# The count product of a routed expert layer: operands on 16 partitions, or on all 128

## The chip, the cores and the metric

One core of one Trainium2 chip runs the whole kernel. The metric is the device time of one execution in microseconds, over several runs; the profile is of one further execution. TensorE (PE) has its own queue, with weight loads shown apart (PEld); VectorE is DVE, ScalarE is ACT, GpSimd is POOL, and SyncE (SP) issues most DMAs.

## The reference, cut to what matters

```python
h = tokens(x, W, class_token, pos_embed)            # 16 images, 197 rows each
h = concatenate([h, txt], axis=1)                   # 16 x 325 rows of 192
h = h + attention(layernorm(h))                     # decay mask, no softmax
y = layernorm(h).reshape(T, 192)                    # T = 5200
sig = sigmoid(y @ Wg.T)                             # 128 experts
topk_idx = top_k(sig + e_bias, 6)                   # 6 experts for each row
order = argsort(topk_idx.reshape(-1))               # rows of each expert in order
pos = arange(P) - starts[se]                        # place within the expert
# each expert takes its first CAP = 192 rows
gu = einsum('ech,ehf->ecf', y[token_buf], W_gate_up)
yb = einsum('eci,eih->ech', silu(g) * u, W_down) * w_buf
out = h + scatter_add(yb) + silu(y @ Wsg) * (y @ Wsu) @ Wsd
```

## The kernel before, in words

The kernel has two stages. The image stage runs over 16 images: patch product, attention, layer norm, router logits, choice of six experts. For each image TensorE's `running_counts` (L1105) turns the 0/1 choices into a running count of rows per expert, and ScalarE makes of it `countT` (experts x 326), which is stored as row `crow[e, image, :]` in DRAM. A column holds 200 less the count so far, so the last column of an image is the first of the next.

The expert stage finds the rows of each active expert from these counts. SP's `load_counts` brings `crow[e]`, a tile of 16 images x 326 columns in bf16, to one of two buffers `counts`. VectorE's `slot_images` (L1593, L1595) compares its first and last column with 192 slot numbers and writes `image`, 16 x 192 in bf16: a 1 where this slot's row lies in this image. TensorE's `count_rows` multiplies, in two halves h of 96 slots each, `image` (the weights) with `counts` (the moving operand), so that each slot gets the count row of its image; the contraction runs over the 16 images. VectorE's `slots` (L1601, tile `le`) counts the columns below the slot number, which is the row's place in the image, and `slot_tokens` (L1608 to L1614, with a register load from `order` ahead) makes the row's number of it. POOL's `get_tokens` gathers the rows, TensorE's `turn_rows` transposes them.

A loop then runs over pairs of active experts. Every engine has its instructions of one iteration (`together`) written out by hand, and they meet by semaphores. TensorE's order in iteration j is: four times `gate_up(j, 0, m)` and `s_up(m)` (the shared experts, for 384 rows), `turn_rows(j, 1)`, **`count_rows(j, 3, 0)`**, `s_up(4)`, `down(j, 0, 0)`, **`count_rows(j, 3, 1)`**, `down(j, 0, 1)`, `gate_up(j, 1, 0)`, `s_up(5)`, `gate_up(j, 1, 1)`, `s_up(6)`, `gate_up(j, 1, 2)`, `s_up(7)`, `gate_up(j, 1, 3)`, `s_down(0)`, `turn_rows(j, 2)`, **`count_rows(j, 4, 0)`**, `s_down(1)`, `down(j, 1, 0)`, **`count_rows(j, 4, 1)`**, `s_down(2)`, `down(j, 1, 1)`. So counts are made for experts one or two places ahead of those being computed.

The waits of TensorE that matter here: `s_up(m)` waits until `s_mul(m-1)` on VectorE (L1657, tile `s_inter`) has emptied the banks of `s_up(m-1)`; `s_down(t)` waits until `s_sum(t-1)` (L1672, tile `s_rows`) has emptied its bank; `count_rows(.., h)` waits for the `le` that read the bank before it. On VectorE, `slots(j, 3, 1)` is followed by `slot_tokens(j, 3)`, `slot_images(j, 4)`, `weigh(j, 0)`, `gated(j, 1, 0)`, `s_lo_part(4)` and `s_mul(5)`.

Before the loop, the same work for experts 0 to 2 lies between three chunks of shared rows (six count products). All L1190 matmuls are `gate_up`, L1220 `s_up`, L1239 to L1246 `s_down`, L1202 `down`, L1171 and L1172 `turn_rows`, L1030 the patch product, L1077 the attention scores.

At the start, POOL sets a row of tiles to constants and raises `pool_set` to 2 after the last of them; the other engines wait for that before they touch such tiles. SBUF is handed out by `Region`: the tiles of the expert stage (`lists`) begin where tiles of the image stage have ended their life, so they lie over memory that the image stage uses.

Of the kernel before, what the change touches and what calls it, by code (L numbers as in the profile page):

```python
# [20 lines left out]
BF16 = mybir.dt.bfloat16  # L21
# [5 lines left out]
B = 16  # L27
# [9 lines left out]
SP = S + 1  # L37
# [6 lines left out]
CAP = 192  # L44
# [15 lines left out]
PACKED_BANKS = (0, 6, 5, 2, 7, 0, 1, 2)  # L60
PACKED_FREE = (0, 0, 0, 0, 0, 1, 0, 4)
BEHIND = (T - BASE) // WIDTH
AHEAD_TILES = sum(t for _, _, t in AHEAD)
ROWS = T + CAP + WIDTH
TOGETHER = E + 1
# [20 lines left out]
def wait(eng, sem, value):  # L86

    if isinstance(value, int) and value <= 0:
        return
    eng.wait_ge(sem, value)  # L90


def wait_apart(eng, passed, *waits):


    for sem, v in waits:
        if not isinstance(v, int) or v > 0:
            eng.wait_ge(sem, v)
            eng.sem_inc(passed, 1)
# [7 lines left out]
def build(nc, xp, txt, wtok, wgu, wdn, wsg, wsu, wsd, w_first, c_base, c_late,  # L107
          c_cum, c_up, c_ident, c_iota, c_ecol, c_rest, c_rest_col, c_tables, out):
    yw = nc.dram_tensor("yw_rows", (T + CAP, YW), F32, kind="Internal").ap()
    crow = nc.dram_tensor("count_rows", (E, B, SP), BF16, kind="Internal").ap()  # L110
    acc = out

    with ExitStack() as ctx:
        def keep(name, shape, dt=F32):
            return ctx.enter_context(nc.sbuf_tensor(name, shape, dt))

        def sem(name):
            return ctx.enter_context(nc.semaphore(name))
# [17 lines left out]
        rest_row = keep("rest_row", [B, CAP])  # L136
# [16 lines left out]
        sb = Region(start).place  # L153

        images = Region(start)
        sb = images.place
# [85 lines left out]
        sb = chunks.place  # L242
# [11 lines left out]
        sb = experts.place  # L254
# [8 lines left out]
        sb = weights_split.place  # L263
        gu_hi = [sb(f"gu_hi{p}", [128, 2, 2 * I], F32R) for p in range(2)]
        gu_lo = [sb(f"gu_lo{p}", [128, 2, 2 * I], F32R) for p in range(2)]
        lists = Region(max(weights_split.at, from_counts))
        sb = lists.place
# [6 lines left out]
        pick = sb("pick", [128, E])  # L274
        order = sb("order", [1, LIST], I32)
        n_active = sb("n_active", [1, 1], I32)
        counts = [sb(f"counts{p}", [B, SP], BF16) for p in range(2)]
        reach = sb("reach", [B, CAP])
        image = sb("image", [B, CAP], BF16)
        le = sb("le", [CH, S], BF16)  # L280
        before = sb("before", [CH, 2])
        tok = sb("tok", [CH, 2])
# [5 lines left out]
        x_rows = [sb(f"x_rows{p}", [CH, 2, YW]) for p in range(2)]  # L288
        w_slot = [sb(f"w_slot{p}", [CH, 2]) for p in range(2)]
        y_rows = sb("y_rows", [CH, 2, D])  # L290


        tok_ps, pv_ps, pv2_ps, lg_ps, ct_ps = psum[0], psum[1], psum[2], psum[3], psum[4]
# [95 lines left out]
        cr_in = [sem(f"cr_in{p}") for p in range(2)]  # L389
# [40 lines left out]
        def load_order(eng, n):  # L430
            return eng.value_load(order[0:1, bass.ds(n, 1)], min_val=0, max_val=E - 1)
# [8 lines left out]
        def load_first(eng, n_act):  # L440

            return eng.value_load(tables[0:1, bass.ds(n_act + TOGETHER, 1)], min_val=K // 2, max_val=BEHIND - 1)

        def load_more(eng, n_act):
            return eng.value_load(tables[0:1, bass.ds(n_act + MORE, 1)], min_val=0, max_val=E // 2 - BEHIND + 1)

        def arrivals(j, n, p, per):

            return j * per + ((n - p) // 2 + 1) * per

        def tiles_before(o):

            if isinstance(o, int) and o <= N_AHEAD:
                return sum(t for _, _, t in AHEAD[:o])
            return AHEAD_TILES + (o - N_AHEAD) * TILES

        with nc.Block() as block:
            @block.sync
            def _(sp):
# [108 lines left out]
                def load_counts(j, n, first=False):  # L568
                    if not first:
                        wait_apart(sp, passed, (cnt_mm, 4 * j + 2 * n - 2))  # L570
                    e = load_order(sp, 2 * j + n)
                    sp.dma_start(counts[n % 2][:, :], crow[e, :, :]).then_inc(cr_in[n % 2], 16)

                def load_weights(j, n, first=False):
                    if not first:
# [14 lines left out]
                sp.wait_ge(order_ready, 1)  # L590
                sp.wait_ge(ct_out, 16 * B)
                load_counts(0, 0, True)
                load_counts(0, 1, True)
                store_weights(B - 1)
                sp.wait_ge(pv_mm, B)
# [4 lines left out]
                act_n = load_active(sp)  # L600
                pairs = load_pairs(sp, act_n)
                load_counts(0, 2)
                load_counts(0, 3)
                with sp.Fori(0, pairs) as j:
# [7 lines left out]

                wait_apart(sp, passed, (added, pairs * (PER_PAIR - 16) + ADDED_AHEAD + 16 * BEHIND))

# [11 lines left out]
            def _(pool):  # L626
# [3 lines left out]
                pool.memset(patches[:, :, 0:1], 0.0)  # L630
                pool.memset(patches[:, :, IMG:], 0.0).then_inc(pool_set, 1)
                pool.memset(half_neg[:, :], -0.5)
                for c in norm:
                    pool.memset(c["mv"][:, :, :], 1.0)
                    for name in ("hiA", "loA", "st"):
                        pool.memset(c[name][:, :].bitcast(F32), 0.0)
# [55 lines left out]
                def add_shared(o, so_far, row, width, tiles):  # L692

                    wait_apart(pool, passed, (added, so_far), (s_rows_ready, tiles_before(o) + tiles))
                    r = width // tiles
                    pool.dma_start(acc[bass.ds(row, width), :].rearrange("(t p) n -> p t n", p=r), s_rows[0:r, 0:tiles, :],  # L696
                                   accum_op=ALU.add).then_inc(added, 16)
# [14 lines left out]
                with pool.Fori(0, pairs) as j:  # L712
# [5 lines left out]
                    add_shared(j + N_AHEAD, PER_PAIR * j + 64 + ADDED_AHEAD, row, WIDTH, TILES)  # L718
                with pool.Fori(first_k, BEHIND) as k:
                    n_before = k + more_k  # L720
# [5 lines left out]
            def _(act):  # L726
# [161 lines left out]
                def s_alone(o, so_far, width, tiles):  # L888
# [5 lines left out]
                    for t in range(tiles):  # L894
                        s_half(o, so_far, width, tiles, t, True)

                _, width, tiles = AHEAD[0]
                last = B - 1
                turned(last)
# [33 lines left out]
                s_half(0, 0, width, tiles, 0, PACKED)  # L933
                s_half(0, 0, width, tiles, 1, PACKED)
                _, width, tiles = AHEAD[1]
                s_hi_part(1, width, 0)
                s_silu(1, width, 2, ALONE)
# [31 lines left out]
                def together(j):  # L969
                    o = j + N_AHEAD  # L970
                    silu(j, 0, 0)
                    s_silu(o, WIDTH, 0)
                    gu_part(j, 1, 0)
                    silu(j, 0, 1)
                    s_silu(o, WIDTH, 1)
                    s_hi_part(o, WIDTH, 0)
                    silu(j, 0, 2)
                    s_silu(o, WIDTH, 2)
                    s_hi_part(o, WIDTH, 1)
                    gu_part(j, 1, 1)  # L980
                    silu(j, 0, 3)
                    s_silu(o, WIDTH, 3)
                    s_hi_part(o, WIDTH, 2)
                    split_x(j, 1)
                    s_silu(o, WIDTH, 4)
                    s_hi_part(o, WIDTH, 3)
                    silu(j, 1, 0)
                    s_hi_part(o, WIDTH, 4)
                    s_silu(o, WIDTH, 5)
                    gu_part(j, 2, 0)  # L990
                    silu(j, 1, 1)
                    s_silu(o, WIDTH, 6)
                    s_hi_part(o, WIDTH, 5)
                    silu(j, 1, 2)
                    s_silu(o, WIDTH, 7)
                    s_hi_part(o, WIDTH, 6)
                    s_hi_part(o, WIDTH, 7)
                    silu(j, 1, 3)
                    s_half(o, PER_PAIR * j + ADDED_AHEAD, WIDTH, TILES, 0)
                    split_x(j, 2)  # L1000
                    gu_part(j, 2, 1)
                    s_half(o, 0, WIDTH, TILES, 1)
                    s_half(o, 0, WIDTH, TILES, 2)

                with act.Fori(0, pairs) as j:
                    together(j)
                with act.Fori(first_k, BEHIND) as k:
                    n_before = k + more_k
# [3 lines left out]
            def _(pe):  # L1012
# [238 lines left out]
                def s_alone(o, at, width, tiles, rows_out):  # L1251
                    data = moving(at, width)
                    for m in range(SM):
                        s_up(o, data, width, m, True)
                    for t in range(tiles):
                        s_down(o, width, tiles, t, True, bank_free=(y_ready, rows_out) if t == 1 else None)
# [115 lines left out]
                wait_apart(pe, passed, (inter_ready, pairs * 8))  # L1372
                with pe.Fori(first_k, BEHIND) as k:
                    s_alone(k + more_k + N_AHEAD, k * WIDTH + BASE, WIDTH, TILES, pairs * 2 + 1)

            @block.vector
            def _(dve):
# [210 lines left out]
                def slot_images(j, n):  # L1588

                    dve.wait_ge(cr_in[n % 2], arrivals(j, n, n % 2, 16))  # L1590
                    wait(dve, cnt_mm, 4 * j + 2 * n)
                    own = counts[n % 2]
                    dve.tensor_scalar(reach[:, :], rest_row[:, :], own[:, 0:1], None, ALU.is_le).then_inc(reach_ready, 1)  # L1593
                    dve.wait_ge(reach_ready, 2 * j + n + 1)
                    dve.scalar_tensor_tensor(image[:, :], rest_row[:, :], own[:, SP - 1:SP], reach[:, :],  # L1595
                                             ALU.is_gt, ALU.mult).then_inc(image_ready, 1)

                def slots(j, n, h):
# [353 lines left out]
```

## Time and profile before

| | |
|---|---|
| median of 3 runs | 711.11 us (708.4 to 711.25) |
| the profiled execution, its own time | 710.25 us |
| its span, first to last instruction | 708.6 us |
| mean granted TensorE clock | 0.988 |
| TensorE busy | 675.0 us (95%) |
| weight loads | 630.5 us (89%) |
| VectorE busy | 471.5 us (67%) |
| ScalarE busy | 331.9 us (47%) |
| GpSimd busy | 210.5 us (30%) |

"Busy" is the time in which at least one instruction of the engine runs. Matmuls are pipelined: one is recorded from its start to its modelled end and the next starts before that, so the distance between two starts is what a matmul costs the queue, not its duration. A timeline row gives start, duration, engine, line, operation, output and inputs, and after "x" how many instructions of one kind were merged; square brackets hold the idle time of the engine before it and who ended it.

### The profile page before, as it was taken

The numbers are of one execution on the slowest core, as the hardware profiler recorded it, in microseconds if no ns is written. First come the engines' busy times: TensorE is split into PE (matmuls) and PEld (weight loads), VectorE is DVE, ScalarE is ACT, GpSimd is POOL, SyncE is SP. The second block draws the span as 40 slices with busy tenths as digits, with TensorE's granted clock in tenths as the row PEclk, the third lists the DMA queues.
The fourth block names the chain that finished last, engine by engine and source line by source line (L and its number), as shares of the span: only waits on it lengthen the run. The fifth ranks groups of instructions, "written<-read, shape, count | busy, mean of one in ns | idle before, by whom it ended". The sixth has DMA issues, their size and how long they took to land.

```text
span 708.6 us, 16559 instructions
## 1 busy us (share of the span) xinstructions
PE 675.0 (95%) x4587; PEld 630.5 (89%) x4588; DVE 471.5 (67%) x1486; ACT 331.9 (47%) x803; POOL 210.5 (30%) x312
## 2 busy tenths in 40 slices
PE   6979999999999999999999999999999999999993
PEld 6879988999989888889999999999999999999993
DVE  2357788887888888666576666666666666666651
ACT  1335555645556565444444444444444444444431
POOL 3113223232233300310333333333333324242430
PEclk9989999999999999999999999999999999999998
DMA  8136344544444232621454544445464545454531
GB/s 280 44 101 218 112 131 144 172 131 136 145 136 144 88 104 54 181 71 25 99 110 99 110 99 102 108 99 111 97 113 97 113 97 113 97 113 97 113 56 20
DMA packets 74180, 79.36 MB, mean 112 GB/s; under 512 B 6361, under 2 KB 65897, under 8 KB 74154
## 3 DMA queue, kind: packets, MB, share of 16 engines
q1 hardware_dynamic: 61706, 65.81, 33.1%
q0 software_dynamic: 12160, 12.60, 11.0%
q10 hardware_dynamic: 288, 0.66, 0.3%
q8 instruction: 10, 0.16, 0.1%
q14 instruction: 16, 0.13, 0.1%
HBM read 51.73 MB, written 19.32 MB: 100 GB/s over the span
## 4 chain that ended last, share of the span: by engine, by line
PE 67%; DVE 12%; DMA 8%; issue 7%; ACT 2%; POOL 1%; DVEq 1%; POOLq 0%; ACTq 0%; SPq 0%
PE bank L1220 19%; PE bank L1030 9%; PE bank L1190 9%; PE bank L1239 7%; PE bank L1018 6%; PE bank L1202 6%; DMA result<-y_rows,put_idx 5%; PE bank L1060 3%; PE bank L1240 3%; DMA result<-s_rows 1%; DVE s_inter L1657 1%; DVE stats L1387 1%; PE bank L1088 1%; DVE w_raw L1483 1%; DVE h L1411 1%
## 5 line engine op out<-in xcount | busy, mean ns | idle before, releaser
L1657 DVE TENSOR_TENSOR s_inter<-s_gate,bank 128x384 f32<-128x384 f32 (+1 forms) x112 | 60.3, 539 | 68.7 <-PE bank L1220 58.8
L1239 PE MATMUL bank<-s_dn,s_in_hi 128*128 128x384 f32 (+1 forms) x287 | 87.3, 365 | 3.3 <-DVE s_rows L1672 3.0
L865 ACT ACTIVATE s_gate<-bank 128x384 f32<-128x384 f32 (+1 forms) x112 | 53.5, 479 | 67.7 <-PE bank L1220 67.7
L1030 PE MATMUL bank<-w_tok,patches 128*128 128x192 f32 x384 | 72.7, 343 | 8.2 <-DMA patches<-xp 6.9
L689 POOL DMA_INDIRECT result<-y_rows,put_idx x40 | 65.4, 1635 | 38.1 <-DVE y_rows L1644 15.3
L1220 PE MATMUL bank<-all_hiA,s_hi 128*128 (+4 forms) x210 | 73.5, 350 | 2.0 <-DVE s_inter L1657 0.6
L760 ACT ACTIVATE y<-h,shift,rstd 128x192 f32<-128x192 f32 (+2 forms) x96 | 45.6, 538 | 59.4 <-POOL shift L623 59.4
L1030 PEld LDWEIGHTS bank<-w_tok,patches 128*128 128x128 f32 x384 | 65.7, 200 | 8.1 <-issue 8.1
L1240 PE MATMUL bank<-s_dn,s_in_lo 128*128 128x192 f32 (+1 forms) x287 | 72.0, 251 | 0.0
L1220 PE MATMUL bank<-all_B,s_lo 128*128 (+4 forms) x210 | 70.1, 334 | 0.0
L1220 PE MATMUL bank<-all_B,s_hi 128*128 (+4 forms) x210 | 70.1, 334 | 0.0
L1220 PE MATMUL bank<-all_loA,s_hi 128*128 (+4 forms) x210 | 69.9, 333 | 0.0
L1220 PE MATMUL bank<-all_hiA,s_lo 128*128 (+4 forms) x210 | 69.8, 332 | 0.0
L857 ACT ACTIVATE gate<-bank 116x192 f32<-116x192 f32 x80 | 26.5, 332 | 89.4 <-PE bank L1190 88.1
L1239 PEld LDWEIGHTS bank<-s_dn,s_in_hi 128*128 128x128 f32 (+1 forms) x287 | 53.6, 187 | 8.0 <-DVE s_rows L1672 5.2
L1202 PE MATMUL bank<-down_w,inter 116*96 116x192 f32 x320 | 59.3, 328 | 0.0
L618 POOL TENSOR_SCALAR ve<-mv 128x3 f32<-128x3 f32 x32 | 9.5, 296 | 158.1 <-DVE mv L1391 158.1
L1240 PEld LDWEIGHTS bank<-s_dn,s_in_lo 128*128 128x128 f32 (+1 forms) x287 | 54.5, 190 | 0.0
L1665 DVE TENSOR_TENSOR s_in_lo<-s_inter,s_in_hi 128x384 fp32r<-128x384 f32 (+1 forms) x98 | 52.6, 537 | 0.7 <-ACT s_in_hi L873 0.6
L679 POOL DMA_INDIRECT x_rows<-yw_rows,get_idx x46 | 44.1, 958 | 27.3 <-POOL get_idx L675 20.3
L696 POOL DMA_DIRECT2D result<-s_rows x14 | 19.9, 1418 | 106.0 <-DMA result<-y_rows,put_idx 72.6
L1202 PEld LDWEIGHTS bank<-down_w,inter 116*96 116x96 f32 x320 | 49.7, 163 | 1.7 <-issue 0.3
(205 smaller groups left out, 1846.4 us busy)
## 6 DMA issues: line engine op xcount, KB each, us to landing
raw_gu<-wgu SPq DMA_DIRECT2D x22, 464.0 KB, 5.0
raw_gu<-wgu SPq DMA_DIRECT2D x44, 232.0 KB, 5.9
patches<-xp SPq DMA_DIRECT2D x16, 588.0 KB, 4.4
down_w<-wdn SPq DMA_DIRECT2D x22, 348.0 KB
result<-s_rows POOLq DMA_DIRECT2D x13, 288.0 KB
result<-h SPq DMA_DIRECT2D x16, 192.0 KB
yw_rows<-y SPq DMA_DIRECT2D x16, 192.0 KB
all_hiA<-y_hiA SPq DMA_DIRECT2D x16, 162.5 KB, 2.6
```

The lines of the kernel that those rows point to most:

```text
L679: pool.indirect_dma_start(x_rows[p][:, h, :], None, yw[:, :], bass.IndirectOffsetOnAxis(ap=get_idx[p][:, h:h + 1], axis=0)).then_inc(x_in[ ...
L689: pool.indirect_dma_start(acc[:, :], bass.IndirectOffsetOnAxis(ap=put_idx[:, h:h + 1], axis=0), y_rows[:, h, :], None, compute_op=ALU.add) ...
L760: ins = act.activation(c["y"][0:r, t, 0:D], h[0:r, t, :], ACT.Identity, bias=c["shift"][0:r, t:t + 1], scale=c["rstd"][0:r, t:t + 1])
L865: act.activation(s_gate[m % 2][0:r, 0:width], up_banks(m, alone)[0][0:r, 0:width], ACT.Silu).then_inc(s_gate_ready, 1)
L1030: mm = pe.matmul(tok_ps[:, t * D:(t + 1) * D], own[:, c, t * 128:(t + 1) * 128], w_tok[:, c, :], start=c == 0, stop=c == KC - 1)
L1190: mm = pe.matmul(ps, w, x[:, :], start=i == 0, stop=i == 4)
L1202: mm = pe.matmul(dn_ps[0:CH, h * D:(h + 1) * D], inter[:, m, rows], down_w[n % 2][:, m, :], start=m == 0, stop=m == EM - 1)
L1220: mm = pe.matmul(ps[0:r, 0:width], w, x, start=i == 0, stop=i == 4)
L1239: pe.matmul(bank[0:r, 0:2 * D], s_in_hi[:, m, rows], s_dn[:, m, :], start=m == 0, stop=False)
L1240: pe.matmul(bank[0:r, 0:D], s_in_lo[:, m, rows], s_dn[:, m, 0:D], start=False, stop=False)
L1657: dve.tensor_tensor(s_inter[m % 2][0:r, 0:width], s_gate[m % 2][0:r, 0:width], up, ALU.mult).then_inc(s_inter_ready, 1)
L1665: dve.tensor_tensor(lo_part, s_inter[m % 2][0:r, 0:width], hi_part.bitcast(F32), ALU.subtract).then_inc(s_lo_ready, 1)
```

## The change

The two `counts` buffers and `image` become 128 partitions high and are placed in a region of their own, at byte 227616 of each partition, above the memory of both the image stage and the lists. POOL sets them to zero at the start, ahead of `pool_set` 2. SP's load and VectorE's `slot_images` still write and read their 16 real rows only. The line of `count_rows` is the same, but it names the whole tiles, so its contraction now runs over 128 rows, of which 112 are zero.

```diff
+FROM_TOP = 227616
...
-        counts = [sb(f"counts{p}", [B, SP], BF16) for p in range(2)]
         reach = sb("reach", [B, CAP])
-        image = sb("image", [B, CAP], BF16)
...
+        top = Region(FROM_TOP)
+        counts = [top.place(f"counts{p}", [128, SP], BF16) for p in range(2)]
+        image = top.place("image", [128, CAP], BF16)
+        assert max(lists.at, images.at) <= FROM_TOP, (lists.at, images.at)
...
-                    sp.dma_start(counts[n % 2][:, :], crow[e, :, :]).then_inc(cr_in[n % 2], 16)
+                    sp.dma_start(counts[n % 2][0:B, :], crow[e, :, :]).then_inc(cr_in[n % 2], 16)
...
+                for own in (*counts, image):
+                    pool.memset(own[:, :], 0.0)
...
-                    own = counts[n % 2]
+                    own = counts[n % 2][0:B, :]
...
-                    dve.scalar_tensor_tensor(image[:, :], rest_row[:, :], own[:, SP - 1:SP], reach[:, :],
+                    dve.scalar_tensor_tensor(image[0:B, :], rest_row[:, :], own[:, SP - 1:SP], reach[:, :],
```

## Rows read from the trace of the kernel before

**Rows 1.** Busy time of each engine in two stretches; PEclk is the granted TensorE clock
```profile
20.00:50.00 30.00, 24.92 (x137) 22.72 (x138) 13.12 (x41) 10.13 (x25) 5.59 (x14) 0.83 0.20 59
...
317.00:677.00 360.00, 355.59 (x2447) 338.32 (x2446) 233.21 (x589) 159.99 (x361) 123.21 (x127) 1.00 0.47 99
```

**Rows 2.** Tile `image`, the count product: nanoseconds min/median/max
```profile
L1164 PE MATMUL bank<-counts,image x46: 305/334/335, 281.9 to 673.8; 16*96 16x326 bf16 x46
```

**Rows 3.** Timeline of PE, count product 284.11: start, duration, what
```profile
283.84 0.34 PE L1220 MATMUL bank<-all_B,s_lo 128*128 128x384 f32 x1
284.11 0.33 PE L1164 MATMUL bank<-counts,image 16*96 16x326 bf16 x1
284.37 0.44 PE L1220 MATMUL bank<-all_hiA,s_hi 128*128 128x384 f32 x1
284.65 0.34 PE L1220 MATMUL bank<-all_hiA,s_lo 128*128 128x384 f32 x1
284.82 0.34 PE L1220 MATMUL bank<-all_loA,s_hi 128*128 128x384 f32 x1
```

**Rows 4.** Timeline of PE around product (3,1)
```profile
439.94 1.46 PE L1202 MATMUL bank<-down_w,inter 116*96 116x192 f32 x8
441.34 0.33 PE L1164 MATMUL bank<-counts,image 16*96 16x326 bf16 x1
441.60 1.54 PE L1202 MATMUL bank<-down_w,inter 116*96 116x192 f32 x8
442.85 0.39 PE L1190 MATMUL bank<-x_hiA,gu_hi 128*116 128x192 f32 x1
```

**Rows 5.** The load behind (4,1), a run of L1202 without a break, the page's L1202
```profile
458.47 0.19 PEld L1239 LDWEIGHTS bank<-s_dn,s_in_hi 128*128 128x128 f32 x1 [0.15 <-issue]
...
460.67 1.47 PE L1202 MATMUL bank<-down_w,inter 116*96 116x192 f32 x8
461.83 0.39 PE L1190 MATMUL bank<-x_hiA,gu_hi 128*116 128x192 f32 x1
...
L1202 PE MATMUL bank<-down_w,inter 116*96 116x192 f32 x320 | 59.3, 328 | 0.0
```

**Rows 6.** Timeline of PE in the image stage, L1105 (running counts)
```profile
176.44 0.33 PE L1030 MATMUL bank<-w_tok,patches 128*128 128x192 f32 x1
176.60 0.42 PE L1105 MATMUL bank<-cum,chosen 128*128 128x326 bf16 x3
176.87 0.52 PE L1077 MATMUL bank<-q_A,yT_A 128*128 128x325 f32 x1
```

**Rows 7.** Timeline of weight loads, first of s_up(6)
```profile
446.68 0.19 PEld L1220 LDWEIGHTS bank<-all_hiA,s_hi 128*128 128x128 f32 x1
```

**Rows 8.** Timelines at (3,0), DVE and weight load, and at (4,0), PE
```profile
437.41 0.56 DVE L1657 TENSOR_TENSOR s_inter<-s_gate,bank 128x384 f32<-128x384 f32 x1 [0.47 <-PE bank L1220]
...
438.08 0.19 PEld L1220 LDWEIGHTS bank<-all_hiA,s_hi 128*128 128x128 f32 x1 [0.33 <-issue]
...
454.61 0.45 PE L1239 MATMUL bank<-s_dn,s_in_hi 128*128 128x384 f32 x1 [0.30 <-DVE s_rows L1672]
```

**Rows 9.** Timeline of DVE behind (3,1)
```profile
441.71 0.55 DVE L1601 TENSOR_SCALAR_CACHE_REDUCE le<-bank,rest 96x325 bf16<-96x325 f32 x1 [0.30 <-PE bank L1164]
...
443.24 0.16 DVE L1608 TENSOR_TENSOR tok<-before,tok_base 96x2 f32<-96x2 f32 x1 [0.97 <-DVE le L1601]
...
445.98 0.54 DVE L1657 TENSOR_TENSOR s_inter<-s_gate,bank 128x384 f32<-128x384 f32 x1
```

**Rows 10.** Timeline of DVE before the loop, expert 2
```profile
300.76 0.31 DVE L1593 TENSOR_SCALAR reach<-rest_row,counts 16x192 f32<-16x192 f32 x1 [1.85 <-DMA counts<-count_rows]
```

**Rows 11.** Timeline of POOL at the start
```profile
4.26 0.42 POOL L641 MEMSET choice<- 128x390 f32 x1
...
10.21 0.34 POOL L649 COPY h<-txt 69x192 f32<-69x192 f32 x1 [5.46 <-DMA txt<-txt]
```

**Rows 12.** Timeline of POOL in the loop
```profile
532.62 0.18 POOL L675 COPY get_idx<-slot_tok 96x2 int32 x1 [6.32 <-DVE slot_tok L1614]
```

## The prediction

> **What bounds the kernel now.** I read the page first (table above), then the stretches, then the count products, then the instructions around four of them in order of time. In the loop over pairs of experts, 317 to 677 us, the matmul engine is busy for 355.59 of 360 us at a granted clock of 1.00 [rows 1]. So the loop, half of the kernel, is TensorE's queue end to end, and a tenth of a microsecond taken from that queue comes off the end, unless TensorE then meets a wait that it now just misses. The tail hangs on the loop too: the last shared product ends, its rows are added and stored.
>
> The change touches one kind of matmul, the count product of L1164: 46 of them, 334 ns by their record, 16 rows [rows 2]. Six stand before the loop (experts 0 to 2, two halves each) and 40 in it, so the loop has ten iterations of four products: I call them (3,0), (3,1), (4,0), (4,1), by the `count_rows` call.
>
> What one costs is not its 334 ns but what it does to the starts around it. Product at 284.11 [rows 3]: the matmul before it started at 283.84, so 0.27 us pass where neighbours of its kind take 0.17 (284.65 to 284.82). From the product to the next matmul 0.26 pass, though 326 columns at 2.4 GHz are 0.14. The next one, 0.28 before its successor, again against 0.17. Excess: 0.10 + 0.12 + 0.11 = about 0.33 there, in a stretch without a wait. In the loop, eight `down` matmuls lie on each side of (3,1) [rows 4]: 439.94 to 441.34 is 1.40 for eight starts; in a run that nothing breaks, from 460.67, eight last 1.47 of which the last takes 0.33, so seven gaps are 1.14, one is 0.163 and eight are 1.30 [rows 5]. Before the product 0.10 too much, product to next 0.26 instead of 0.14, and after it 1.25 to the L1190 at 442.85 instead of the 1.16 to the L1190 at 461.83. Sum 0.10 + 0.12 + 0.09 = 0.31. Behind (4,1) too the weight load sat idle for 0.15 with no releaser [rows 5]; I take the same excess there.
>
> Is that the price of 16 rows? The same form of product with full rows is in the image stage: `running_counts`, bf16, 326 + 198 + 70 columns, first two with 128 rows. It starts 0.16 after the L1030 before it, the unbroken pitch of that kind, and its three matmuls take 0.27 to the next engine work, 594 columns at 2.4 GHz being 0.25 [rows 6]. No gap ahead, none between. L1202, with 116 rows between neighbours of 128, has none either beyond those beside the product [rows 5]. So I read the excess as the price of going from (nearly) full rows to 16 and back, not of bf16 or of an odd row count.
>
> The Trainium skill has a rule for it (TensorEngine Tiling (Array Packing), Key Properties and When to Use Tiling): changing the tiling mode, 32-row tiles belonging to a contraction of 32, drains the engine. Rows 3 to 5 agree, and by the rule the sum would be the one below. The Trainium skill also has a rule against this change (TensorE: Matmul & The Clock Gate, LDWEIGHTS): the contraction rows do not matter to the time of a weight load. By that the sum would be nought; rival 2 has its mechanism from the rows.
>
> **The change part by part.**
> (a) Rows of the product, 16 to 128. Columns and weight columns stay, so nothing is added to the stream. Removed where TensorE does not wait: 0.10 + 0.12 + 0.09 = 0.31. Not all: the f32 weight load after the product (0.19 for L1220 [rows 7]) was overlapped by a 0.34 matmul and would lie beside 0.14 of product, leaving some 0.05. I take 0.26, bounds 0.22 and 0.31.
>
> (b) Which of the four are free of waits:
> (4,1): no wait on either side, next wait of TensorE is in the following iteration and fed by TensorE itself. 0.26.
> (3,0): the next matmul, s_up(4), waits for s_mul(3), which started 437.41 on the end of s_up(3) [rows 8]; the product lies in that shadow. 0.
> (4,0): the next, s_down(1), waits for the evacuation of s_down(0): 454.61, ended by `s_rows` on DVE [rows 8]. 0.
> (3,1): frees 0.26 too, but what is late next is DVE. Its chain starts with `le`, which reads this product, at 441.71; then the register load in `slot_tokens` holds the queue until `tok` at 443.24; from there `slot_images`, `weigh`, `gated`, `s_lo_part` run without a gap until s_mul(5) at 445.98 [rows 9]. TensorE's s_up(6) waits for that s_mul(5): its weights load at 446.68, 0.70 after s_mul(5) started [rows 7], and in (3,0), a place where TensorE did wait, that distance is 438.08 - 437.41 = 0.67 [rows 8]. So there is 0.03 of slack now: DVE and TensorE arrive together. The chain itself comes earlier by the gap ahead of the product, 0.10, and perhaps 0.03 of the product's own latency. TensorE can thus move 0.10 + 0.03 + 0.03 = 0.16 of its 0.26. Bounds: 0.09 (no latency gained, and part of a weight load left open by the wait; a load fully open costs 0.11, 284.37 to 284.65 against the 0.17 of its kind [rows 3]) and 0.26 (chain follows fully). I take 0.16.
>
> An iteration: 0.26 + 0.16 = 0.42; ten: 4.2. Bounds (0.22 + 0.09) x 10 = 3.1 and (0.31 + 0.31) x 10 = 6.2.
>
> (c) The six before the loop. Those of experts 0 and 1 gain something, but DVE then waits for the count row of expert 2, which lands at 300.76 by its own DMA [rows 10], and TensorE waits behind that: absorbed. Two products follow, expert 2's: the first gives 0.26; the second waits for the `le` that reads the first, so I count the part behind it alone, the 0.12 + 0.09 less the 0.05. I take 0.4, bounds 0.2 and 0.6.
>
> (d) Three memsets on POOL ahead of `pool_set` 2: the dearest memset there is 0.42 [rows 11], so at most 1.3 us, and as bf16 tiles of 326 and 192 columns nearer 0.6. POOL's next work is the text copy at 10.21, and before it POOL sat idle for 5.46, for a DMA [rows 11]; the consumers of `pool_set` 2 come later. Cost 0; without that cover, 1.3.
>
> (e) The new address and the smaller slices: DVE's `reach` and `image` and SP's DMA keep 16 rows and their sizes. 0. The pool around it: POOL waits 6.32 us per iteration for `slot_tok` [rows 12], so its chain of adds has the room that 0.6 per iteration would need. 0.
>
> Sum: 4.2 + 0.4 = 4.6, bounds 3.3 and 6.8. The profiled execution took 710.25 (span 708.6), which would give 705.6; it lies 0.9 below the median of the runs, 711.11, so the forecast against that is **706.5**.
>
> **Rivals.**
> 1. *The DVE chain does not hold* (3,1): it is shortened with the product, or the slack is larger than 0.03. Then both products give 0.26 to 0.31: 5.2 to 6.2, plus 0.4 to 0.7: about 704.7. For it: `tok` follows a register load whose time may shift. Against: s_mul(5) started back to back.
> 2. *Rows do not matter*: the gaps come from the small bf16 product between f32 ones with waits on its weight load, and stay: 711.1. For it: the full-row product of rows 6 is in another stage, starts behind f32 work of one kind only and has 128 weight columns, so nothing there shows it between L1202 and L1239. Against: rows 6, and waits already met cost L1190 and L1220 nothing like it.
> 3. *The gain is taken back by further DVE or ACT waits*, as TensorE's waits for s_inter are all fed with little room: half of it goes, 2.1 + 0.2: 708.8. Against: the other waits follow TensorE's own matmuls and move with them.
> 4. *Slower: the clock.* 46 products light all rows; from 20 to 50 us this kernel had a granted clock of 0.83 [rows 1], after a stretch with idle TensorE. A drop to 0.98 over the loop would cost 360 x 0.02 = 7.2 and end at 713.7; it decides from 1.3% on (4.6 of 360). Against: the loop is already at 1.00 with 128 rows nearly everywhere, four products stream for 0.56 of an iteration's 36 us.
>
> **Numbers.** Forecast 0.60, rival 1 0.14, rival 2 0.10, rival 3 0.12, rival 4 0.04. The bound of what can be told is 0.5%, 3.6 us. The forecast's 4.6 with its bounds from 3.3 lies above it mostly: faster 0.55 of its 0.60, and rival 1 wholly; rivals 2 and 3 are no change. Faster 0.69, same 0.27, slower 0.04. Range 704.0 to 709.3: down to rival 1 with its best bounds, up to rival 3, leaving out rivals 2 and 4 (0.14) and a little besides.
>
> **What would show it.** The products of L1164 with 128 rows start 0.16 after the L1202 before them and 0.14 to 0.17 before the next matmul at (3,1) and (4,1); the iteration takes 0.42 less than before; TensorE shows a new wait at s_up(6) on `s_inter`; (3,0) and (4,0) keep their distance to what follows. The prediction is wrong if the gaps around the 128-row product stay (rival 2), if an iteration loses 0.5 or more (rival 1), or 0.2 or less (rival 3).

## The result, and the profile after

The changed kernel takes 703.28 us (median of 4 runs, 702.04 to 703.68) against 710.31 for the kernel before (708.4 to 711.25, 4 runs): ratio 0.990, 95% interval 0.9877 to 0.9923. It is 7.0 us faster by the medians, where 4.6 were forecast, and 0.7 us below the lower end of the forecast range, 704.0. Its profiled execution took 703.68 us, 6.6 less than the one of before. Line numbers from L628 on have moved by 3 to 5: the product is L1169, `down` L1207, `s_up` L1225, `s_down` L1244 to L1251.

The page of the changed kernel, its head, busy times and chain by engine:

```profile
span 702.0 us, 16562 instructions
...
PE 662.6 (94%) x4587; PEld 628.4 (90%) x4588; DVE 471.7 (67%) x1486; ACT 332.0 (47%) x803; POOL 211.4 (30%) x315
...
PE 48%; DMA 18%; issue 11%; DVE 11%; POOL 3%; ACT 3%; SPq 2%; DVEq 1%; POOLq 1%; ACTq 0%
```

Only TensorE's time is less; POOL has three instructions more, the memsets. The chain now goes through DMA for 18%, before it was 8%; most of it is the landing of POOL's adds in the loop. That is no new bound: run e10_fill_moved, below, does the same adds at 34.40 us an iteration, and the changed kernel takes 35.31.

Tile `image` in the changed kernel (minimum, median, maximum in ns) answers to [rows 2]:

```profile
L1169 PEld LDWEIGHTS bank<-counts,image x46: 119/123/123, 281.5 to 667.2; 128*96 128x96 bf16 x46
L1169 PE MATMUL bank<-counts,image x46: 299/303/339, 281.5 to 667.3; 128*96 128x326 bf16 x46
L637 POOL MEMSET image<- x1: 257/257/257, 2.3 to 2.3; 128x192 bf16 x1
```

By its record the product is 0.03 us shorter. What it costs shows in the starts around it. TensorE's timeline at (3,1) and the same product one iteration later:

```profile
437.59 1.46 PE L1207 MATMUL bank<-down_w,inter 116*96 116x192 f32 x8
438.89 0.30 PE L1169 MATMUL bank<-counts,image 128*96 128x326 bf16 x1
439.04 1.46 PE L1207 MATMUL bank<-down_w,inter 116*96 116x192 f32 x8
440.20 0.39 PE L1195 MATMUL bank<-x_hiA,gu_hi 128*116 128x192 f32 x1
...
474.21 0.30 PE L1169 MATMUL bank<-counts,image 128*96 128x326 bf16 x1
```

Against [rows 4]: eight starts before the product take 1.30 instead of 1.40, product to next 0.15 instead of 0.26, eight after it 1.16 instead of 1.25. All three excesses are gone, 0.30 together. At (4,1), 455.46, the `s_down` behind the product starts after 0.04, less than the 0.14 to 0.17 that the prediction named; the second `s_down` matmul comes 0.32 after the product, before 0.54. And the iteration is 474.21 - 438.89 = 35.32 (35.31 to 35.32 in all nine distances of the trace), where it was 35.93 to 35.95 and once 36.03.

TensorE's timeline at (3,0) and (4,0) of the changed kernel:

```profile
435.11 0.24 PE L1177 MATMUL bank<-ident,x_rows 96*64 96x96 f32 x1
435.19 0.30 PE L1169 MATMUL bank<-counts,image 128*96 128x326 bf16 x1
435.76 0.41 PE L1225 MATMUL bank<-all_hiA,s_hi 128*128 x1 [0.27 <-DVE s_inter L1662]
...
451.16 0.25 PE L1177 MATMUL bank<-ident,x_rows 96*64 96x96 f32 x1
451.24 0.30 PE L1169 MATMUL bank<-counts,image 128*96 128x326 bf16 x1
451.97 0.44 PE L1244 MATMUL bank<-s_dn,s_in_hi 128*128 128x384 f32 x1 [0.42 <-DVE s_rows L1677]
```

The product comes 0.09 sooner behind the transposes, and the next matmul waits that much longer for VectorE. These two give nothing.

The account: the loop's first product starts 0.47 earlier than before (329.25 after 329.72), the nine distances between its products (3,0) are together 5.71 shorter, and from the last (3,0) to the end of the span it is 0.37 less. That is the 6.55 by which the spans differ (708.56 and 702.01).

The 0.47 is 0.54 that the two products of expert 2 gave, less 0.08 by which the first of them started later. From that first one to the loop's first product pass 25.13 us, before 25.67; in every run below it is 25.13 to 25.14 where these products sum more than 64 rows, and 25.67 to 25.73 where they sum 16 or 64. When expert 2's first product starts is no measure of the change: it differs from trace to trace (303.5 to 305.8).

### The profile page after: what moved, and what is told of

The parts are those of the page before. It is cut to its first block, busy times and chain, and to the rows that moved or that the text cites. A ratio compares the mean times of both kernels' runs of the same rounds, so it can differ in the third digit from the quotient of the medians.

```text
span 702.0 us, 16562 instructions
## 1 busy us (share of the span) xinstructions
PE 662.6 (94%) x4587; PEld 628.4 (90%) x4588; DVE 471.7 (67%) x1486; ACT 332.0 (47%) x803; POOL 211.4 (30%) x315
## 4 chain that ended last, share of the span: by engine, by line
PE 48%; DMA 18%; issue 11%; DVE 11%; POOL 3%; ACT 3%; SPq 2%; DVEq 1%; POOLq 1%; ACTq 0%
PE bank L1225 11%; DMA result<-y_rows,put_idx 11%; PE bank L1035 8%; PE bank L1023 6%; PE bank L1244 5%; PE bank L1195 5%; DMA result<-s_rows 4%; PE bank L1207 3%; PE bank L1065 3%; PE bank L1245 2%; DVE stats L1392 1%; DMA counts<-count_rows 1%; PE bank L1093 1%; DVE w_raw L1488 1%; DMA txt<-txt 1%
## 5 line engine op out<-in xcount | busy, mean ns | idle before, releaser
L1244 PE MATMUL bank<-s_dn,s_in_hi 128*128 128x384 f32 (+1 forms) x287 | 87.3, 366 | 4.6 <-DVE s_rows L1677 4.3
L1035 PE MATMUL bank<-w_tok,patches 128*128 128x192 f32 x384 | 70.6, 336 | 8.9 <-DMA patches<-xp 6.9
L1225 PE MATMUL bank<-all_hiA,s_hi 128*128 (+4 forms) x210 | 73.4, 349 | 4.0 <-DVE s_inter L1662 4.0
L1035 PEld LDWEIGHTS bank<-w_tok,patches 128*128 128x128 f32 x384 | 63.7, 195 | 8.7 <-issue 8.7
L1225 PE MATMUL bank<-all_B,s_hi 128*128 (+4 forms) x210 | 70.1, 334 | 0.0
L1225 PE MATMUL bank<-all_B,s_lo 128*128 (+4 forms) x210 | 70.1, 334 | 0.0
L1225 PE MATMUL bank<-all_loA,s_hi 128*128 (+4 forms) x210 | 69.9, 333 | 0.0
L1225 PE MATMUL bank<-all_hiA,s_lo 128*128 (+4 forms) x210 | 69.8, 332 | 0.0
L1244 PEld LDWEIGHTS bank<-s_dn,s_in_hi 128*128 128x128 f32 (+1 forms) x287 | 53.7, 187 | 8.4 <-DVE s_rows L1677 6.8
L1207 PE MATMUL bank<-down_w,inter 116*96 116x192 f32 x320 | 58.4, 326 | 0.0
L1207 PEld LDWEIGHTS bank<-down_w,inter 116*96 116x96 f32 x320 | 50.3, 163 | 0.6
```

Source lines behind the costliest of these rows:

```text
L1035: mm = pe.matmul(tok_ps[:, t * D:(t + 1) * D], own[:, c, t * 128:(t + 1) * 128], w_tok[:, c, :], start=c == 0, stop=c == KC - 1)
L1207: mm = pe.matmul(dn_ps[0:CH, h * D:(h + 1) * D], inter[:, m, rows], down_w[n % 2][:, m, :], start=m == 0, stop=m == EM - 1)
L1225: mm = pe.matmul(ps[0:r, 0:width], w, x, start=i == 0, stop=i == 4)
L1244: pe.matmul(bank[0:r, 0:2 * D], s_in_hi[:, m, rows], s_dn[:, m, :], start=m == 0, stop=False)
```

## The experiments

Each was timed beside the kernel before on the same chip. "Iteration" is the distance from one count product to the same one of the next iteration, nine per trace. In the kernel before it is 35.93 to 35.95, once 36.03.

| run | us | before | ratio, 95% interval | iteration |
|---|---|---|---|---|
| changed kernel | 703.28 | 710.31 | 0.990 (0.9877 to 0.9923) | 35.31 |
| e1_place_only | 710.65 | 710.80 | 1.000 (0.9988 to 1.0013) | 35.93 |
| e2_rows64 | 710.87 | 710.80 | 1.000 (0.9988 to 1.0012) | 35.93 to 36.03 |
| e3_rows65 | 703.74 | 710.80 | 0.9903 (0.9879 to 0.9926) | 35.31 to 35.33 |
| e4_full_31 | 707.82 | 710.80 | 0.9963 (0.9932 to 0.9994) | 35.63 to 35.65, once 35.73, once 35.92 |
| e5_delay2 | 703.48 | 710.24 | 0.9905 (0.9881 to 0.9930) | 35.31 |
| e6_delay8 | 703.87 | 710.24 | 0.9902 (0.9877 to 0.9927) | 35.31, once 35.36, once 35.52 |
| e7_fill_3 | 709.70 | 710.24 | 0.9991 (0.9976 to 1.0007) | 35.48 to 36.22 |
| e8_fill_both | 702.41 | 710.24 | 0.9884 (0.9861 to 0.9906) | 34.80 to 35.55 |
| e9_delay_big | 704.85 | 710.56 | 0.9922 (0.9905 to 0.9938) | 35.31, twice 35.8 |
| e10_fill_moved | 693.53 | 710.56 | 0.9762 (0.9745 to 0.9778) | 34.40 |
| e11_full_h1 | 704.11 | 710.56 | 0.9916 (0.9895 to 0.9936) | 35.31 |
| e12_filled_16 | 706.26 | 713.90 | 0.9899 (0.9883 to 0.9916) | 35.50 |

### Which part of the change, and how many rows

Three runs differ from the changed kernel in the rows of the product alone:

```diff
-                    pe.matmul(cnt_ps[0:CH, 0:SP], image[:, h * CH:(h + 1) * CH], counts[n % 2][:, :],
+                    pe.matmul(cnt_ps[0:CH, 0:SP], image[0:rows, h * CH:(h + 1) * CH], counts[n % 2][0:rows, :],
```

**e1_place_only**, rows = 16.

> All of the change but its core: 128-partition tiles, zeros, the place at the top, and a product that still runs over the 16 real rows. Theory 1 (the gap is the switch between 16 rows and full rows): the time of before, 710 us, an iteration of 35.94 us, product to next matmul 0.26 us at (3,1) and (4,1). Rival (the place or the zeros brought the gain): the time of the changed kernel, 703 us, an iteration of 35.31.

710.65 us against 710.80, and an iteration of 35.93. The place at the top and the zeros bring nothing, and the memsets cost nothing that can be told.

**e2_rows64**, rows = 64.

> The changed kernel with the product over 64 rows. Theory 1 in the form that any narrower row tile than the neighbours' pays the switch: gaps as with 16 rows, iteration 35.94, 710 us. Rival 1b (only the smallest tile, up to 32 rows, pays): no gaps, 35.31, 703 us. Rival 1c (the gap shrinks with the rows in proportion): about half, 35.7, 707 us.

**e3_rows65**, rows = 65.

> The changed kernel with the product over 65 rows, one more than the run with 64. Theory 1: over half of the rows is the same tile as full rows, as the 96 and 116 rows of neighbouring matmuls suggest: no gaps, iteration 35.31, 703 us. Rival (all 128 rows are needed, or the gap goes in proportion): 35.6 or more, 706 us or more.

Tile `image` and the timelines of TensorE and of its weight loads (PEld) at (3,1), first with 64 rows:

```profile
L1170 PE MATMUL bank<-counts,image x46: 307/336/337, 281.8 to 673.9; 64*96 64x326 bf16 x46
...
439.85 1.46 PE L1208 MATMUL bank<-down_w,inter 116*96 116x192 f32 x8
441.24 0.34 PE L1170 MATMUL bank<-counts,image 64*96 64x326 bf16 x1
441.51 1.38 PE L1208 MATMUL bank<-down_w,inter 116*96 116x192 f32 x7
...
441.24 0.12 PEld L1170 LDWEIGHTS bank<-counts,image 64*96 64x96 bf16 x1 [0.25 <-issue]
441.51 0.57 PEld L1208 LDWEIGHTS bank<-down_w,inter 116*96 116x96 f32 x4
```

then with 65:

```profile
L1170 PE MATMUL bank<-counts,image x46: 303/303/339, 281.6 to 666.8; 65*96 65x326 bf16 x46
...
437.02 1.46 PE L1208 MATMUL bank<-down_w,inter 116*96 116x192 f32 x8
438.32 0.30 PE L1170 MATMUL bank<-counts,image 65*96 65x326 bf16 x1
438.47 1.46 PE L1208 MATMUL bank<-down_w,inter 116*96 116x192 f32 x8
...
438.16 0.12 PEld L1170 LDWEIGHTS bank<-counts,image 65*96 65x96 bf16 x1
438.32 0.79 PEld L1208 LDWEIGHTS bank<-down_w,inter 116*96 116x96 f32 x5
```

One row more changes 1.39 to 1.30 ahead and 0.27 to 0.15 behind, and 710.9 us to 703.7. The time has nothing to do with how many rows are summed: 16 and 64 cost the same, 65 and 128 cost the same. It is a step between 64 and 65. The PEld rows show where the time goes. With 65 rows each weight load runs ahead of its matmul: the product's load starts 0.16 before the product, the `down` load behind it 0.15 before its matmul. With 64 rows neither load runs ahead: the product's starts with the product, 441.24, and the one behind it with its matmul, 441.51. The Trainium skill (TensorEngine Tiling (Array Packing), Available Configurations and Key Properties) has row tiles of 32, 64 and 128 and says that a change of the mode drains the engine. Both runs agree with it. Whether two narrow products in a row would pay once or twice no run shows. Weight loads were 114 to 117 ns at 16 and 64 rows and 119 to 123 at 65 and 128, so the other rule of the Trainium skill (TensorE: Matmul & The Clock Gate, LDWEIGHTS), that rows do not set a load's time, holds to within 9 ns for the load itself and says nothing of the queue around it.

**e11_full_h1**: full rows in (3,1) and (4,1) alone, `rows = 128 if h == 1 and n > 2 else B`.

> Full rows in products (3,1) and (4,1) alone; (3,0), (4,0) and the six before the loop keep 16 rows. Theory: (3,0) and (4,0) lie in waits and give nothing, so the iteration is that of the changed kernel, 35.31, and only what the six before the loop gave (0.5 us) is missing: 703.8 us. Rival (every product of the loop gives its share): 35.6, 706.8 us.

704.11 us, and 35.31 in each of nine iterations: although (3,0) and (4,0) went back to 16 rows the iteration lost nothing. Where they stand, the switch lies in a wait.

### The step that failed: VectorE's chain behind (3,1)

**e4_full_31**: `rows = 128 if (n, h) == (3, 1) else B`.

> Full rows in product (3,1) of each iteration alone, 16 rows in all others. This is the step on which the prediction rests. As predicted (VectorE's chain behind (3,1) holds, 0.16 us an iteration): iteration 35.78, 708.7 us. Theory now (the chain has slack of 0.45 us in most iterations and the one I read was an exception with a long register load): 0.29 us an iteration, 35.65, 707.4 us.

Seven of nine iterations take 35.63 to 35.65, so (3,1) alone gives 0.29 to 0.31, not the 0.16 of the prediction. Two take 35.73 and 35.92: in these, and in these alone, the register load in `slot_tokens` lasted 0.86 and 1.04 us (the others 0.30 to 0.60). That refutes the 35.78 of the prediction and fits the 35.65 expected second. VectorE's timeline in the first of the two, `tok` late and `s_inter` of s_mul(5) without idle time before it:

```profile
477.93 0.16 DVE L1614 TENSOR_TENSOR tok<-before,tok_base 96x2 f32<-96x2 f32 x1 [0.95 <-DVE le L1607]
480.67 0.54 DVE L1663 TENSOR_TENSOR s_inter<-s_gate,bank 128x384 f32<-128x384 f32 x1
```

That was also the picture in [rows 9]. But another iteration of the same trace of before, two later, reads:

```profile
514.55 0.16 DVE L1608 TENSOR_TENSOR tok<-before,tok_base 96x2 f32<-96x2 f32 x1 [0.40 <-DVE le L1601]
...
517.86 0.55 DVE L1657 TENSOR_TENSOR s_inter<-s_gate,bank 128x384 f32<-128x384 f32 x1 [0.45 <-PE bank L1220]
```

There VectorE waited 0.45 us for TensorE. The load took 0.30 to 0.31 in six of the ten iterations and 0.75 to 1.02 in four; I had read one of the four (0.88). In the one with 1.02 the iteration itself took 36.03.

In the changed kernel VectorE still waits there, 0.27 to 0.33 us in nine of ten iterations; the first two rows are one of these. In the tenth the load took 0.70, VectorE did not wait, and the iteration was 35.31 all the same:

```profile
440.20 0.16 DVE L1613 TENSOR_TENSOR tok<-before,tok_base 96x2 f32<-96x2 f32 x1 [0.40 <-DVE le L1606]
...
443.32 0.56 DVE L1662 TENSOR_TENSOR s_inter<-s_gate,bank 128x384 f32<-128x384 f32 x1 [0.31 <-PE bank L1225]
...
369.96 0.16 DVE L1613 TENSOR_TENSOR tok<-before,tok_base 96x2 f32<-96x2 f32 x1 [0.79 <-DVE le L1606]
372.70 0.55 DVE L1662 TENSOR_TENSOR s_inter<-s_gate,bank 128x384 f32<-128x384 f32 x1
```

The wait at s_up(6) that the prediction named as a sign is not in this trace. The next runs measure the rest of the room by putting memsets of dead tiles between `slot_tokens(j, 3)` and `slot_images(j, 4)`.

```diff
                     slot_tokens(j, 3)
+                    dve.memset(pick[:, 0:64], 0.0)
+                    dve.memset(pick[:, 64:128], 0.0)
                     slot_images(j, 4)
```

**e5_delay2**: as above.

> The changed kernel with two small memsets of a dead tile (about 0.2 us together) in VectorE's queue right behind slot_tokens(j, 3), so in the chain that ends in s_mul(5). As predicted (no slack once the product gives its 0.26): every 0.1 costs 1 us, so 705 us or more. Theory now: VectorE sits idle for 0.31 us before s_mul(5) in the changed kernel, the memsets fit into that: iteration 35.31, 703.3 us.

Free: 703.48 us and 35.31; the idle time before s_mul(5) went from 0.32 or 0.33 to 0.26 in most iterations (0.31 to 0.23 in the one shown).

**e6_delay8**: eight memsets of 16 columns.

> The same with eight memsets (0.5 to 0.8 us together). Theory now: the idle 0.31 and 0.03 of slack at TensorE are used up and the rest comes onto TensorE's queue: 0.2 to 0.5 us an iteration more, 705 to 708 us, and TensorE's first load of s_up(6) waits for s_inter. Rival (VectorE's chain is not tied to TensorE there at all): 703.3.

They added 0.23 us, less than I had put, and left some 0.1 of the idle time. They cost 0.05 and 0.21 us in two iterations, those in which the register load took 0.57 and 0.73, and nothing in the rest. 703.87 us can't be told from the changed kernel.

**e9_delay_big**: `spare` of 448 columns and all of `pick`.

> The changed kernel with two larger memsets (448 and 128 columns, 0.55 to 0.6 us together) of dead tiles in VectorE's queue behind slot_tokens(j, 3). Theory: 0.31 us of VectorE's idle time before s_mul(5) and some 0.04 at TensorE take up the first part; what is over, about 0.2 to 0.25 us an iteration, comes onto TensorE: 35.5 to 35.6, 705.5 us, with the first load of s_up(6) waiting. Rival (no tie to TensorE): 703.5 us.

VectorE's and TensorE's timelines in one of its two long iterations:

```profile
441.05 0.16 DVE L1614 TENSOR_TENSOR tok<-before,tok_base 96x2 f32<-96x2 f32 x1 [0.94 <-DVE le L1607]
441.24 0.16 DVE L1617 SCALAR_TENSOR_TENSOR past<-tok,slot_no 96x2 f32<-96x2 f32 x1
441.54 0.16 DVE L1620 TENSOR_TENSOR slot_tok<-tok,past 96x2 f32 x1
441.74 0.43 DVE L1829 MEMSET spare<- 128x448 f32 x1
442.14 0.17 DVE L1830 MEMSET pick<- 128x128 f32 x1
...
444.17 0.54 DVE L1663 TENSOR_TENSOR s_inter<-s_gate,bank 128x384 f32<-128x384 f32 x1
...
444.85 0.41 PE L1226 MATMUL bank<-all_hiA,s_hi 128*128 x1 [0.25 <-DVE s_inter L1663]
```

My 0.2 to 0.25 an iteration did not come: the memsets added 0.4 net (the `reach` behind them got shorter), which the idle time just took up, and seven iterations stayed at 35.31. Where a long register load, 0.85, came on top, the iteration took 0.49 more, and TensorE's first matmul of s_up(6) waits for `s_inter`. So the tie that the prediction described exists, and its room can be worked out: what load and memsets took beyond a load of 0.30, less what the iteration lost. It is 0.44 to 0.46 in all of these: e4 (0.56 less 0.10, 0.74 less 0.29), e6 (0.50 less 0.05, 0.66 less 0.21), e9 (0.93 less 0.49). With 16 or 64 rows it was 0.61 to 0.63 (loads of 0.99 to 1.02 cost 0.08 to 0.10 in the kernel before and in e2). The load of 0.88 that I had read left some 0.04 of that, near the 0.03 of the prediction, but a load of 0.30 leaves all of it.

That the loads were short in the changed kernel's trace is no part of the change's design. Had the four long ones of before (0.75 to 1.02) come again, the ten iterations would have lost some 0.5 us together, an estimate from the room of 0.45.

### Filling the waits that (3,0) and (4,0) lie in

**e7_fill_3**: `down(j, 0, 0)` goes ahead of `s_up(4)`.

```diff
                     count_rows(j, 3, 0)
+                    down(j, 0, 0)
                     s_up(o, data, WIDTH, 4)
-                    down(j, 0, 0)
                     count_rows(j, 3, 1)
```

> The changed kernel with down(j, 0, 0) moved ahead of s_up(4), into the wait behind product (3,0) where neither 16 nor 128 rows mattered. Theory: that wait is 0.57 us from product to s_up(4), of which the product itself needs 0.14; with down in it, 0.4 to 0.5 us an iteration go: 34.85, 698.5 us. Rival (the wait moves to s_up(5) or to the y_rows chain): 703 us.

709.70 us: the 698.5 expected did not come. The wait of 0.27 us behind (3,0) was filled and a longer one, 0.44 to 1.19, came up at s_up(6) in each of the ten iterations. VectorE and TensorE in one of them:

```profile
441.06 0.56 DVE L1606 TENSOR_SCALAR_CACHE_REDUCE le<-bank,rest 96x325 bf16<-96x325 f32 x1
...
442.54 0.16 DVE L1613 TENSOR_TENSOR tok<-before,tok_base 96x2 f32<-96x2 f32 x1 [0.92 <-DVE le L1606]
...
445.29 0.53 DVE L1662 TENSOR_TENSOR s_inter<-s_gate,bank 128x384 f32<-128x384 f32 x1
...
445.97 0.42 PE L1225 MATMUL bank<-all_hiA,s_hi 128*128 x1 [0.94 <-DVE s_inter L1662]
```

Product (3,1) now follows s_up(4) directly, so `le` comes behind `s_mul(4)` and `s_lo_part(3)`, 1.4 us after the product (439.64) instead of 0.35. The chain of the failed step binds here in every iteration, and the iteration follows the register load one for one: it is 35.18 to 35.20 plus that load, from 35.48 at 0.30 to 36.22 at 1.03.

**e8_fill_both**: also `down(j, 1, 0)` ahead of `s_down(1)` and `down(j, 1, 1)` ahead of `s_down(2)`.

> As the run before, and in the second half down(j, 1, 0) ahead of s_down(1) and down(j, 1, 1) ahead of s_down(2). The wait of 0.73 us behind product (4,0) is filled, but s_down(2) comes only 0.8 us behind s_down(1), whose evacuation takes 1.1 to 1.2: about 0.3 of it returns. 0.4 more an iteration than the run before: 34.45, 694.5 us. Rival (the evacuations pace the three s_down and everything returns): 698.5 us.

702.41 us, where 694.5 were expected: 34.80 to 35.55 an iteration, with the same wait at s_up(6), 0.44 to 1.19. Both waits that were filled are gone. The long register loads are now those ahead of `slot_weights` in the same queue:

```profile
440.15 0.17 DVE L1626 COPY w_slot<-x_rows 96x2 f32 x1 [0.80 <-issue]
```

The iteration is 34.50 to 34.53 us plus that load, which took 0.30 in one iteration and 0.56 to 1.04 in nine.

**e10_fill_moved**: e8, and two pieces leave that chain on VectorE.

```diff
                     slots(j, 3, 1)
-                    slot_tokens(j, 3)
-                    slot_images(j, 4)
                     weigh(j, 0)
...
                     gated(j, 1, 1)
+                    slot_images(j, 4)
                     s_mul(o, WIDTH, 6)
...
                     gated(j, 1, 2)
+                    slot_tokens(j, 3)
                     s_mul(o, WIDTH, 7)
```

> The run with both fills, and on VectorE slot_images(j, 4) moved behind gated(j, 1, 1) and slot_tokens(j, 3) behind gated(j, 1, 2), out of the chain between product (3,1) and s_mul(5), which made TensorE wait 1.2 us at s_up(6) there. Theory: that chain is what took the fills' gain back; without it an iteration takes 34.3 to 34.5 us, 694 us. Rival (the waits come back at s_up(7), whose s_mul(6) now has slot_images ahead of it, or at s_down(2)): 700 us or more.

693.53 us, ratio 0.9762: the fastest version, 2.4% below the kernel before. Iterations of 34.40, and no idle time above 0.04 us between TensorE's matmuls in the loop. The register loads ahead of `slot_weights` are as long as in e8, 0.52 to 1.02 in eight of ten iterations, and cost nothing here.

**e12_filled_16**: the same with products over 16 rows.

> The fastest version so far (both waits filled, two pieces of VectorE's chain moved, 693.5 us, 34.40 us an iteration) with the count products over 16 rows again. There all four products of an iteration stand in TensorE's queue without a wait beside them. Theory: each costs the 0.3 us of the row switch again, so 1.2 us an iteration and 12 us in the loop, some 0.5 before it: iteration 35.6, 706 us, twice of what the change gave to the kernel as it was. Rival (only (3,1) and (4,1) matter, whatever stands around the others): 35.0, 700 us.

TensorE's timeline at the products (3,0) and (3,1), e10_fill_moved:

```profile
432.31 0.30 PE L1169 MATMUL bank<-counts,image 128*96 128x326 bf16 x1
432.45 1.46 PE L1207 MATMUL bank<-down_w,inter 116*96 116x192 f32 x8
```

and e12_filled_16:

```profile
436.31 0.33 PE L1169 MATMUL bank<-counts,image 16*96 16x326 bf16 x1
436.58 1.54 PE L1207 MATMUL bank<-down_w,inter 116*96 116x192 f32 x8
```

35.50 against 34.40: 1.10 us an iteration, four products at 0.275. At each of the four the time ahead of the product is 0.09 longer and product to next 0.12. The two ran on different chips, so the ratios to before are compared: 0.9899 to 0.9762 is 1.4% of the time, some 9.7 us by the medians, and 7.5 to 12 by the ends of the intervals; the spans of the two traces differ by 11.5. 12.5 were expected; the 6.5 of the rival lies below all of these. In this order of work the change is worth 1.10 us an iteration, in the order it was made in 0.63.

## Why the prediction was wrong

Its direction was right, its size too small by 2.4 us by the medians (2.0 by the profiled executions), and the range ended 0.7 above the time.

**Where the excess comes from: right.** 0.31 around (3,1) and a fast full-row form by [rows 6]; e2 and e3 show the step between 64 and 65 rows, e1 that nothing else in the change matters. Rival 2 (rows do not matter) is refuted by e3.

**(a) The price of a product: mis-sized.** "I take 0.26": 0.30 at (3,1) and 0.32 at (4,1). The 0.05 set aside for a weight load left open beside the short product did not come; product to next is 0.15 at (3,1). That is 0.10 an iteration, 1.0 us: 0.6 of it at (4,1), and 0.4 at (3,1), which are part of the 1.4 below.

**(b) (3,0) and (4,0): right**, 0 and 0 (e11). **(4,1): right** but for its size. **(3,1): the failed step.** "So there is 0.03 of slack now: DVE and TensorE arrive together ... I take 0.16." The slack was that of one iteration with a long register load. In six of ten VectorE sat idle for 0.45 us ahead of s_mul(5), the room was 0.61 to 0.63, and (3,1) gave its 0.30 whole (e4: 0.29 to 0.31). That is 0.14 an iteration, 1.4 us; 1.0 of it would have been missed at the price of 0.26 too. The reckoning itself came out where its premise held: e4's iteration with a load of 0.86 gained 0.20 and not 0.30. Rival 1 described what happened (5.2 to 6.2 plus 0.4 to 0.7) and had 0.14; it even named the register load whose time may shift, and the other nine iterations of the trace already in hand would have told.

**(c) to (e): right.** The loop begins 0.47 earlier (0.4 forecast, bounds 0.2 and 0.6). The two products of expert 2 gave 0.54, so the second gave as much as the first and not half of it; the first of them started 0.08 later than before. e1 shows the memsets and the place at no cost, and e10's 34.40 with the same adds on POOL that POOL set no bound. Rival 3 and rival 4 did not happen: the granted clock is 0.989 after 0.988.

**The last 0.8.** The forecast of 706.5 lies 3.2 above the measured 703.28. 0.8 of that is no matter of the change: the forecast was set against a median of 711.11 from three runs, with a fourth it is 710.31. Against that the forecast would be 705.7 and the lower end of the range 703.2, so 703.28 would lie just inside. The sum stays too small all the same: the loop was forecast at 4.2 (bounds 3.1 and 6.2) and gave 6.1 (5.71 + 0.37).

The sum that the traces give is 0.47 + 5.71 + 0.37 = 6.55, against the forecast's 0.4 + 4.2.

## What to carry to other kernels

Here a small matmul with 16 or 64 contraction rows between matmuls of 96 to 128 rows cost TensorE about 0.3 us beyond its own columns; zero rows up to 65 or 128 removed that, for one memset per tile at the start. Count it only at the places where TensorE does not wait: two of four here gave nothing until the waits around them were filled, and then all four did. And before one row of a loop is used as a slack, read the same row in several iterations: the iteration read here was one of four exceptions in ten, and that cost 1.0 to 1.4 of the 2.4 us missed.

## What the hardware showed that I had not expected

The register load from SBUF in VectorE's queue does not always take the same time. In the kernel before (line, queue, ns minimum, median, maximum):

```profile
L431 DVEq TENSOR_LOAD <-order x44: 298/304/1024, 286.0 to 674.3; - x44
```

In the traces of all fourteen kernels every such load in the loop above 0.33 us, up to 1.04, began between 0.3 and 1.7 us after POOL had finished issuing its add of shared rows (L696, a direct DMA with addition); those that began sooner or later took 0.30 to 0.32. In e8, e10 and e12, where the order of work is another, the long loads are those ahead of `slot_weights` and no longer those in `slot_tokens`. The one behind the failed step:

```profile
439.75 1.40 POOL L696 DMA_DIRECT2D result<-s_rows  x1 [7.42 <-DMA result<-y_rows,put_idx]
```

It ended at 441.15 and the load began 0.7 us later. In the iteration at 514 the issue ran to 513.56 and the load began 0.15 after it, with 0.30 us. That this is the cause was not tested: no run moved the add or the load alone.
